# Four message-passing layers on one core: the first layer's scatter in steps of eight tiles in place of four

## The reference

```python
xw = feature @ weight
msgs = edge_weight[:, None] * xw[edge_col]                       # edge_col = dst
agg = segment_sum(msgs, edge_row, num_segments=N)                # edge_row = src
new_feature = agg + bias                                         # then batch norm, relu, residual
```

## Time and profile before

| | us |
|---|---|
| three runs | 6917.25, 6935.78, 6934.15 (median 6934.15) |
| the profiled execution's own time | 6949.26 |
| its span, from the first to the last instruction | 6947.5 |
| PE, its weight load, DVE busy | 3252.0, 2775.7, 2632.2 |
| ACT, POOL busy | 648.9, 3938.1 |
| POOL's 816 scatter DMAs of stage 0a (line 632) busy | 800.8 |
| idle time of POOL before them | 520.5 |

### The profile page before, as it was taken

The page is one execution under the profiler, slowest core; times in us unless marked ns, Lnnn a source line. Parts: engine busy times, 40 slices in busy tenths (PEclk is TensorE's granted clock), DMA queues, the critical chain, the costliest instruction groups (busy, mean ns, idle before and its releaser), DMA issues.

```text
span 6947.5 us, 72488 instructions
## 1 busy us (share of the span) xinstructions
PE 3252.0 (47%) x15507; PEld 2775.7 (40%) x15508; DVE 2632.2 (38%) x4819; ACT 648.9 (9%) x1748; POOL 3938.1 (57%) x3545
## 2 busy tenths in 40 slices
PE   6644444444663333233444444445654444444466
PEld 5533333334652222222344333435633333333365
DVE  6732222224452233233311111138753333333876
ACT  2100000000001000000111111100011111111000
POOL 1556666662005767676466666646636666666364
PEclk7555555566776555555555555557875555555688
DMA  3211111113422111111233333334434444444342
GB/s 88 107 54 43 41 41 41 41 41 100 146 94 101 44 45 45 44 46 44 59 88 89 88 88 89 88 64 141 141 100 126 126 124 127 125 125 127 94 150 92
DMA packets 408304, 599.95 MB, mean 86 GB/s; under 512 B 70191, under 2 KB 291256, under 8 KB 406768
## 3 DMA queue, kind: packets, MB, share of 16 engines
q1 hardware_dynamic: 283842, 315.22, 14.6%
q0 software_dynamic: 119808, 278.86, 14.3%
q10 hardware_dynamic: 4318, 2.92, 0.2%
HBM read 405.45 MB, written 194.43 MB: 86 GB/s over the span
## 4 chain that ended last, share of the span: by engine, by line
another core or an unknown queue 20%; PE 15%; issue 13%; DVE 6%; DVEq 3%; ACT 2%; DMA 1%; ACTq 0%; POOL 0%; POOLq 0%; SPq 0%
PE psG L866 5%; PE psA L898 4%; PE psT L862 2%; PE psA L1044 1%; DVE acc L1081 1%; ACT onehot L722 1%; DVE work L1166 1%; DVE work L1151 1%; DVE onehot L1075 1%; DVEq L232 1%; PE psT L898 1%; DVE work L1597 1%; DVEq L1081 0%; ACT idx_ring L725 0%
## 5 line engine op out<-in xcount | busy, mean ns | idle before, releaser
L866 PE MATMUL psG<-nodes,onehot 128*128 x3264 | 774.0, 412 | 1348.9 <-ACT onehot L722 705.9
L866 PEld LDWEIGHTS psG<-nodes,onehot 128*128 128x128 f32 x3264 | 663.6, 302 | 1499.6 <-issue 1499.6
L667 POOL DMA_INDIRECT work<-kv_table,idx_ring x816 | 836.7, 1025 | 487.8 <-issue 275.6
L650 POOL DMA_INDIRECT work<-rel_table,idx_ring x816 | 843.5, 1034 | 451.5 <-issue 347.3
L632 POOL DMA_INDIRECT msgs<-work,idx_ring x816 | 800.8, 981 | 520.5 <-DVE idx_ring L1460 276.3
L667 POOL DMA_INDIRECT work<-gat_table,idx_ring x816 | 839.2, 1028 | 437.9 <-issue 268.3
L1044 PE MATMUL psA<-work,onehot 128*128 128x128 f32 x1632 | 394.8, 418 | 831.4 <-DVE onehot L1075 548.8
L898 PE MATMUL psA<-work,onehot 128*128 128x136 f32 (+1 forms) x4432 | 655.2, 313 | 192.5 <-DVE acc L1081 116.6
L541 POOL TENSOR_TENSOR work<-work,scores 128x1024 f32<-128x1024 f32 x204 | 485.3, 2400 | 429.5 <-PE psA L898 139.6
L898 PEld LDWEIGHTS psA<-work,onehot 128*128 128x128 f32 x4432 | 623.8, 221 | 221.8 <-issue 219.6
L1044 PEld LDWEIGHTS psA<-work,onehot 128*128 128x128 f32 x1632 | 338.8, 307 | 888.0 <-DVE onehot L1075 548.6
(11 more groups left out here) (279 smaller groups left out, 2504.7 us busy)
## 6 DMA issues: line engine op xcount, KB each, us to landing
rows_seq<-work SPq DMA_DIRECT2D x408, 256.0 KB
work<-rows_seq SPq DMA_DIRECT2D x204, 512.0 KB, 3.4
work<-msgs SPq DMA_DIRECT2D x102, 516.0 KB, 4.0
msgs<-work,idx_ring POOLq DMA_INDIRECT x816
work<-rel_table,idx_ring POOLq DMA_INDIRECT x816
work<-gat_table,idx_ring POOLq DMA_INDIRECT x816
work<-kv_table,idx_ring POOLq DMA_INDIRECT x816
rel_table<-work SPq DMA_DIRECT2D x25, 512.0 KB, 2.6
```

Of the source, the lines that this page charges most:

```text
L650: nc.gpsimd.indirect_dma_start(row_ring[:, s, :], None, rel_table, bass.IndirectOffsetOnAxis(ap=idx_ring[:, s:s + 1], axis=0), bounds_chec ...
L667: nc.gpsimd.indirect_dma_start(ring[:, s, :], None, table, bass.IndirectOffsetOnAxis(ap=idx_ring[:, s:s + 1], axis=0), bounds_check=table. ...
L866: ins = nc.tensor.matmul(psG[:, k % 2, j, 0:width], onehot_t[:, k % 2, j, :], rows(regs[4 * k + j]), start=True, stop=True)
```

## The change

Stage 0a goes in steps of eight tiles: one instruction of 128 x 1024 in place of two of 128 x 512 for the one-hots, ACT's copy and the product with the weights, and one signal where there were two at each handover. PE's eight transposes go to `psA`, which the stage did not use (two turns of half its space), and the eight products to `psT` and `psG` in turn, two PSUM areas that held two quads each. The copied transposes go to a new place in `work` behind the ring. POOL waits once for eight tiles and issues eight DMAs. The loops of PE and ACT still have a body of 16 tiles, DVE's and POOL's one of 48. The starting numbers of the later stages are adapted.

```diff
+        oht0 = SPAN * MSG + AHEAD * HALF
+        onehot_th = work[:, oht0:oht0 + 2 * HALF * P].rearrange("p (r j c) -> p r j c", j=HALF, c=P)
+        ps_turn = psA[:, :, :].rearrange("p s (t c) -> p (s t) c", c=P)
+        ps_halves = [psT[:, :, :, :].rearrange("p a b c -> p (a b) c"), psG[:, :, :, :].rearrange("p a b c -> p (a b) c")]
...
                 for k in range(QUADS):
-                    pool.wait_ge(quad_rdy, g * QUADS + (k + 1))
+                    if k % 2 == 0:
+                        pool.wait_ge(quad_rdy, g * RING + (k // 2 + 1))
...
             with act.Fori(0, BODIES) as g:
-                for k in range(4):
-                    onehots_out("0a", g, k)
+                for h in range(2):
+                    act.wait_ge(tr_done, g * 2 + (h + 1))
+                    nc.scalar.activation(onehot_th[:, h, :, :], ps_turn[:, HALF * h:HALF * h + HALF, :], ACT.Copy)\
+                        .then_inc(oht_rdy, 1)
...
-            fetch("0a", lambda r: nodes[:, bass.ds(r, 1), :], F)
+            with pe.Fori(0, BODIES) as g:
+                regs = blocks_of(ENG.PE, 0, g * BODY, BODY)
+                for h in range(2):
+                    pe.wait_ge(oh_rdy, g * 2 + (h + 1))
+                    for j in range(HALF):
+                        ins = nc.tensor.transpose(ps_turn[:, HALF * h + j, :], onehot[:, h, j, :], ident)
+                    ins.then_inc(tr_done, 1)
+                    pe.wait_ge(oht_rdy, g * 2 + (h + 1))
+                    for j in range(HALF):
+                        ins = nc.tensor.matmul(ps_halves[h][:, j, :], onehot_th[:, h, j, :],
+                                               nodes[:, bass.ds(regs[HALF * h + j], 1), :], start=True, stop=True)
+                    ins.then_inc(got, 1)
...
-            one_hots(0, 0)
+            def half_hots(first, h):
+                V.tensor_tensor(onehot[:, h % 2, :, :], rep(iota[:, :], HALF),
+                                bc(dst_local[:, bass.ds(first, HALF)], P), ALU.is_equal).then_inc(oh_rdy, 1)
+            half_hots(0, 0)
             def messages(g):
-                for k in range(QUADS):
-                    wait_if(dve, tr_done, g * QUADS + (at_quad["0a"] + k))
-                    one_hots(g * SPAN + 4 * (k + 1), k + 1)
-                    dve.wait_ge(got, g * QUADS + (at_quad["0a"] + k + 1))
-                    wait_if(dve, quad_out[k], g * (16 * QUAD))
-                    V.tensor_tensor(msg_ring[:, 4 * k:4 * k + 4, 0:F], psG[:, k % 2, :, :],
-                                    bc(weight[:, bass.ds(g * SPAN + 4 * k, QUAD)], F), ALU.mult)
-                    V.tensor_copy(msg_ring[:, 4 * k:4 * k + 4, F], src_f[:, bass.ds(g * SPAN + 4 * k, QUAD)])
-                    V.tensor_copy(idx_ring[:, 4 * k:4 * k + 4], idx_a[:, bass.ds(g * SPAN + 4 * k, QUAD)])\
+                for h in range(RING):
+                    wait_if(dve, tr_done, g * RING + h)
+                    half_hots(g * SPAN + HALF * (h + 1), h + 1)
+                    dve.wait_ge(got, g * RING + (h + 1))
+                    wait_if(dve, quad_out[2 * h], g * (16 * QUAD))
+                    wait_if(dve, quad_out[2 * h + 1], g * (16 * QUAD))
+                    at = slice(HALF * h, HALF * h + HALF)
+                    V.tensor_tensor(msg_ring[:, at, 0:F], ps_halves[h % 2],
+                                    bc(weight[:, bass.ds(g * SPAN + HALF * h, HALF)], F), ALU.mult)
+                    V.tensor_copy(msg_ring[:, at, F], src_f[:, bass.ds(g * SPAN + HALF * h, HALF)])
+                    V.tensor_copy(idx_ring[:, at], idx_a[:, bass.ds(g * SPAN + HALF * h, HALF)])\
                         .then_inc(quad_rdy, 1)
```

More of the change, by code:

```diff
@@ L331, in gnn @@
         at_added = {ph: at + 2 * HALF * (i + 1) for i, (ph, at) in enumerate(at_agg.items())}
-        at_quad = {"0a": 0, "2a": NQ, "3a": 2 * NQ}
+        at_quad = {"2a": NH, "3a": NH + NQ}
         at_half = {"2b": 0, "3b": NH}
         at_idx = {"1": 0, "2a": NQ, "3a": 2 * NQ + 3}
-        at_oh = {"0a": 0, "0b": NQ + 1, "1": NQ + 1 + NH, "2a": 2 * (NQ + 1) + NH, "2b": 3 * (NQ + 1) + NH,
-                 "3a": 3 * (NQ + 1) + 2 * NH, "3b": 4 * (NQ + 1) + 2 * NH}
+        n_oh = NH + 1
+        at_oh = {"0a": 0, "0b": n_oh, "1": n_oh + NH, "2a": n_oh + NQ + 1 + NH, "2b": n_oh + 2 * (NQ + 1) + NH,
+                 "3a": n_oh + 2 * (NQ + 1) + 2 * NH, "3b": n_oh + 3 * (NQ + 1) + 2 * NH}
         squares_at = {1: 0, "bn": 2, 2: 4, 3: 6, 4: 8}
```

## The result

| | before | after |
|---|---|---|
| median of four runs | 6934.97 us (6917.25 to 6935.95) | 6974.83 us (6963.34 to 6980.37) |
| ratio, 95% interval | | 1.0055 (1.0042 to 1.0069) |
| the profiled execution, its span | 6949.26, 6947.5 | 6963.34, 6961.6 |

I forecast 6883 us and gave slower a chance of 0.16. The time lies just above the range that I gave. So I lean on the differences of stages, and only where they come back in a second pair of profiles.

A forecast was written before the change was run, and what follows sets the result against it. Stage 0a was taken as bound by POOL's work plus its waits. Waits -56 and ends +5 give -51 us: 6949 to 6898, less 15 for the median, 6883 us; range 6795 to 6965, the forecast's own 6850 to 6915.

The forecast's parts named there:

- What bounds the kernel: Stage 0a: POOL's own work, 1045 us, plus 50 waits for DVE's index copy, 209.8 us, together 1254.8 us.
- The waits: POOL in stage 0a: 32 waits of 4.8 us in place of 50 of 4.2, so -56 us.
- My lateness of 1 to 10 us: Stage 0a: PE's completion signals arrive 1 to 10 us late while POOL issues scatters without pause, all once it stops.
- ACT 1.02 and DVE 1.23: Longer steps in stage 0a: ACT's copy about 1.02 us, DVE's one-hots and product about 1.23 us each.
- POOL's 0.30 between scatters: POOL's own issue in stage 0a stays at 0.30 us between neighbouring scatters, 244.2 us before.
- The ends: Start and end of stage 0a: first scatter about 4 us later, last step 1 us more, together +5 us.
- With half the copies I would save at most 5 us; I count 0: DVE's small copies lengthening POOL's scatters in stage 0a: halving them counted as 0, with 5 us kept for the range.
- the rule on DVE and POOL: Certain DVE copies lock GpSimd out until they end; judged not to apply to the doubled product, so no cost.
- Nothing else of the kernel is touched: the later stages only start earlier: Stages after 0a: the same durations to within a few us, no term in the sum.
- A: Rival for stage 0a: waits stay 51 and lengthen to 4.8 us, +40 us, 6974 us; chance 0.17.
- B: Rival for stage 0a: four or more halves a burst or hardly any waits, 6851 to 6777 us; chance 0.20.
- C: Rival for stage 0a: late signals grow later by the same amount, 42 waits of 4.9 us, 6934 us; chance 0.15.

The follow-up runs named there:

- a second pair of profiles: The kernel before and the changed kernel, both unchanged, run again on chip Q, where PE's signals come late: 6956.29 against 6998.24 us, 1.0057.
- the finer kernel: Against the changed kernel: DVE in 512-element instructions, first half of the product already freeing POOL, old code placement; 1.0045 and 1.0039 (chip R), 1.0041 (S) to the kernel before.
- the kernel before padded by 128: The kernel before with 128 never-executed instructions added to DVE's stream in a branch not taken: 6276.58 us beside 6266.84 on chip P.

## Why the prediction was wrong, point by point

**What bounds the kernel.** Right for the chip of the profile: POOL's work plus its waits make the stage, before and after. On a chip without late signals POOL's work alone makes it (1053 us; I had computed a floor of 1045).

**The waits: right in size, in part by luck.** Forecast 32 waits of 4.8, 154 us; measured 28 of 5.7, 160.2. The bursts that end in a wait of over 1 us are 24 to 48 tiles. Two misses cancel: the count fell more than I took, and each wait grew by 1.5 in place of 0.6. Of that 0.54 is the product, and the rest fits signals that come later after POOL stops (in the wait shown 3.8 us and not 2.9). Why, stays open; the finer kernel that would have told never met a late chip. My lateness of 1 to 10 us was also wrong: 14.6 us occurred before and 40.2 after.

**ACT 1.02 and DVE 1.23: right** (1.024, 1.225 and 1.219). POOL's 0.30 between scatters holds too (239.7 against 244.2). The ends were too high: the first scatter came 1.6 us later, not 4.

**First step that failed: "With half the copies I would save at most 5 us; I count 0", and the rule on DVE and POOL put aside "so it is not".** The term has the other sign and is +27.2 us. I tried the rule on the one DVE operation that reads PSUM, and not on the one-hots, which go from SBUF to SBUF and stand 102 times at 1.22 us. Rows 6 even held the evidence, the scatter of 1.32 us, which I gave to the small copies; before, 36 of 37 such scatters end on the one-hots. With this term the forecast of the stage, -51, is -24, and -26.6 was measured in the first pair; the second gave -10.3.

**Second step that failed: "Nothing else of the kernel is touched: the later stages only start earlier".** Here I put the later stages at nothing without a reason. Their code is not touched, but its place is: 83 instructions fewer on DVE, 16 more fetches each in 0b and 2b, +40.9 us in the first pair, +38.6 in the second. This is the larger error and has the sign of the result: -24 + 40 is +16 against +14 in the spans.

**The rivals.** A gave 6974 us, and 6974.83 was measured, by accident: its mechanism, 51 waits of 4.8, didn't occur, 28 did. B's bursts of 32 and more occurred, among shorter ones. C is not it either, since the waits fell by 50 us, though what it names, signals that grow later because only POOL's pauses release them, did occur (its sum left the ends out: 42 waits of 4.9 give +1 with them, not -4). None of the three had the mechanism that decided. My own test of the forecast, that the stage should change by the count of waits times their length, fails by the scatters' 27 us, and that the other stages should stay "as before to within a few us" fails in 0b and 2b.

**A better version.** Halves with split one-hots and the loops in their old place beat the kernel before on the late chip by a little (0.9983, 11 us) and the change by 53 us; on P, where nothing is late, they lose 0.17% to the kernel before. There is no kernel here that is better on all chips.

## What to carry to other kernels

When an edit changes the number of instructions of an engine, count how far it moves the loops behind it, and compare the instruction packets of each later stage before and after; the DVE loops of about 560 instructions here fetched 6 to 7 packets on every pass, and one more cost 1 to 2.5 us. Before a DVE operation from SBUF to SBUF is made longer beside indirect DMAs of POOL, price it by the scatters that would start inside it. And ask whether the stall that an edit attacks belongs to the kernel or to the chip of the one profile: here three of the four later chips had none of it.

## What the runs showed of the hardware

- The same kernel takes 6250 to 6281 us on three chips and 6935 to 6956 in the two late series (the first result and chip Q). While POOL streams indirect DMAs there, a signal of PE arrives up to 14.6 us late (in the change 40.2), often only 2.9 to 3.8 us after POOL stops; stages 0a, 1, 2a and 3a take 1255, 1195, 1243 and 1273 us, where those of the kernel before padded by 128 on chip P take 1051, 1072, 1089 and 1096. With SP's plain DMAs the same stage on a late chip shows none.
- An edge of DVE's code inside a loop cost 16 packets of 8 KB in 16 passes, and 15 to 40 us a stage: 18 to 23 on late chips, in 0b up to 40 on chip P. Why one fetch costs 1.1 us on one chip and 2.5 on another is open; DVE's busy time is the same.
- A scatter that starts while a 128 x 1024 comparison of DVE within SBUF runs takes up to 2.0 us in place of 0.97, and ends 0.84 us after the comparison. If it starts within about 0.03 us of it, it takes its 0.97, and the comparison 1.27 us in place of 1.22. Beside a product of the same length that reads PSUM no scatter is lengthened (66 in after, 99 of half the length before).
